# Sums, attributes and maxima moved for four chunks at a time in a four-layer graph network on one core

## What is computed

```
h = x @ enc_node_w + enc_node_b
e = edge_attr @ enc_edge_w + enc_edge_b
def _genconv(h, edge_attr, src, dst, w1, b1, g1, bb1, w2, b2, t):
    msg = jax.nn.relu(h[src] + edge_attr) + EPS_MSG
    m = msg * t
    seg_max = segment_max(m, dst)
    ex = jnp.exp(m - seg_max[dst])
    denom = segment_sum(ex, dst)
    agg = segment_sum(msg * ex / (denom[dst] + 1e-16), dst)
    z = relu(layernorm(((h + agg) @ w1 + b1), g1, bb1))
    return z @ w2 + b2
h = _genconv(h, e, src, dst, ...)
for i in range(1, 4):
    h = h + _genconv(relu(layernorm(h)), e, src, dst, ...)
```

## Time and profile before

| what | us |
|---|---|
| median of three runs (4375.16 to 4376.1) | 4375.87 |
| the profiled execution | 4376.27 |
| its span in the profile | 4374.4 |
| TensorE busy | 2449.6 |
| VectorE busy | 2876.2 |
| ScalarE busy | 1756.3 |
| GpSimd busy | 3117.8 |

### The profile page before, as it was taken

One profiled execution on the slowest core, in us unless ns is written; L12 is line 12 of the kernel. 1 busy time (PEld: TensorE's weight loads), 2 busy tenths in 40 slices (PEclk: granted clock), 3 DMA queues, 4 the chain that ended last, 5 costly groups with the idle time before them and its releaser, 6 DMA issues.

```text
span 4374.4 us, 37023 instructions
## 1 busy us (share of the span) xinstructions
PE 2449.6 (56%) x9731; PEld 1795.5 (41%) x9731; DVE 2876.2 (66%) x3974; ACT 1756.3 (40%) x3407; POOL 3117.8 (71%) x3248
## 2 busy tenths in 40 slices
PE   4566666665455555555455555555555555555554
PEld 3455545554333333333343333333343333333334
DVE  5777777776566666666656666666665666666665
ACT  2444444444334333333333333333333333333334
POOL 3777777777477777777557777777755777777773
PEclk8767677767577776667657666766656676667775
DMA  3444444454233333333223333333322333333332
GB/s 90 133 133 134 139 138 134 133 140 139 86 99 103 108 103 108 104 108 104 94 59 104 108 104 108 103 109 103 108 76 71 108 104 108 104 108 103 108 103 64
DMA packets 307120, 469.62 MB, mean 107 GB/s; under 512 B 169423, under 2 KB 175305, under 8 KB 306892
## 3 DMA queue, kind: packets, MB, share of 16 engines
q1 hardware_dynamic: 200286, 356.83, 23.8%
q0 software_dynamic: 103552, 109.52, 12.4%
q10 hardware_dynamic: 3054, 0.71, 0.1%
HBM read 217.93 MB, written 248.86 MB: 107 GB/s over the span
## 4 chain that ended last, share of the span: by engine, by line
POOL 70%; issue 23%; PE 2%; DVE 2%; DMA 1%; ACT 1%; POOLq 0%; DVEq 0%; ACTq 0%; SPq 0%
POOL zsrc L518 69%; POOL node_sw L529 1%; DMA zsrc<-z_rows,idx_all 1%; PE pT L789 0%; PE pR L886 0%; PE pX L867 0%; PE pX L778 0%; PE pX L711 0%; ACT sq L642 0%; DVE z L1284 0%; DMA node_sw<-sw_rows,row_idx 0%; DMA sw_rows<-sw_out 0%; DMA x_in<-in_x_dram 0%; ACT sw_out L611 0%; DMA z_rows<-z 0%
## 5 line engine op out<-in xcount | busy, mean ns | idle before, releaser
L518 POOL DMA_INDIRECT zsrc<-z_rows,idx_all x3136 | 3019.5, 963 | 1089.0 <-issue 980.1
L778 PE MATMUL pX<-ident,zsrc 128*128 128x128 f32 x2368 | 604.9, 436 | 1296.7 <-DMA zsrc<-z_rows,idx_all 1296.7
L778 PEld LDWEIGHTS pX<-ident,zsrc 128*128 128x128 f32 x2368 | 518.1, 322 | 1595.3 <-DMA zsrc<-z_rows,idx_all 1595.1
L611 ACT ACTIVATE sw_out<-pT 128x512 f32<-128x512 f32 x784 | 424.8, 594 | 1777.5 <-PE pT L789 1773.3
L1108 DVE TENSOR_TENSOR_SCAN S<-decay,S,pX 128x512 f32<-128x512 f32 x296 | 378.6, 1279 | 678.7 <-ACT decay L603 675.0
L789 PE MATMUL pT<-ident,S 128*128 128x128 f32 x1568 | 637.8, 410 | 43.1 <-DVE W L1112 43.1
L789 PE MATMUL pT<-ident,W 128*128 128x128 f32 x1568 | 627.6, 404 | 0.0
L1091 DVE TENSOR_TENSOR_SCAN M<-pR,M,u 128x512 f32<-128x512 f32 x296 | 377.0, 1274 | 286.7 <-ACT u L598 286.7
L596 ACT ACTIVATE r<-pX,edge_b 128x512 f32<-128x512 f32 x296 | 204.8, 692 | 567.0 <-PE pX L778 567.0
L778 PE MATMUL pA<-ident,zsrc 128*128 128x128 f32 x768 | 194.2, 433 | 422.3 <-DMA zsrc<-z_rows,idx_all 422.3
L773 PE MATMUL pX<-attr_pair,edge_w 128*128 128x512 f32 x592 | 416.0, 791 | 12.3 <-ACT attr_pair L590 12.2
(11 more groups left out here) (201 smaller groups left out, 3100.0 us busy)
## 6 DMA issues: line engine op xcount, KB each, us to landing
sw_rows<-sw_out SPq DMA_DIRECT2D x392, 512.0 KB, 2.9
attr_pair<-attr_cols SPq DMA_DIRECT2D x153, 512.0 KB, 4.4
zsrc<-z_rows,idx_all POOLq DMA_INDIRECT x3136, 2.5
attr_in<-in_edge_attr_dram SPq DMA_DIRECT2D x196, 128.0 KB
attr_cols<-attr_pair SPq DMA_DIRECT2D x49, 512.0 KB, 3.2
max_cols<-M SPq DMA_DIRECT2D x49, 256.0 KB, 3.3
z_rows<-z SPq DMA_DIRECT2D x25, 125.0 KB
node_sw<-sw_rows,row_idx POOLq DMA_INDIRECT x100, 2.5
```

What stands on the lines that cost most here:

```text
L518: pool.indirect_dma_start(zsrc[c % RING][:, t4, h, :], None, z_rows, bass.IndirectOffsetOnAxis(idx_all[:, h, t4, c:c + 1].bitcast(U32), 0) ...
L611: act.activation(sw_out[c % 2][:, :, 2 * b:2 * b + 2, :, :].rearrange("p h t s c -> p (t s) h c"), pT[b][:, :].rearrange("p (a h c) -> p a ...
L778: last = pe.matmul(messages_bank(c, first_layer)[:, t4:CH:SUB], zsrc[c % RING][:, t4, :, :].rearrange("p h c -> p (h c)"), ident[:, :], st ...
```

## The change

Stores of sums cover four chunks: sw_out is two buffers of four chunks, 16 KB per partition, and sw_rows is laid out so that a partition's 16 KB are contiguous. The last group has two chunks (98 = 24 x 4 + 2), which are stored one by one, each with 4 KB per partition; the unused half of that group is written once, in layer 0. Attributes are stored and loaded for four chunks (8 KB per partition) in a ring of three such buffers in place of seven pairs, and the maxima of layer 0 are stored for four chunks from an M of four chunks. The loads of the first three groups for the next layer are issued in `end_layer`, behind the seam's two small loads and ahead of the stores of z, after every layer and the last one too. ScalarE waits for a free sums buffer once per four chunks. The row numbers of last edges follow the new layout, which takes more small VectorE operations in node_ends_3. Some scratch tensors of the start now lie in sw_out and xn.

```diff
-attr_pair = [sb(f"attr_pair{b}", [P, 2 * CH]) for b in range(PRING)]
+attr_four = [sb(f"attr_four{b}", [P, FOUR * CH]) for b in range(ARING)]
-M = two("M", [P, 2 * CH + 1])
+M = two("M", [P, FOUR * CH + 1])
-sw_out = two("sw_out", [P, 2, SUB, 2, H])
+sw_out = two("sw_out", [P, FOUR, 2, SUB, 2, H])
...
+            def store_sw(g0, f):
+                sp.wait_ge(back_sb, 2 * g0 + 2 * (FOURS[f][-1] + 1 + PRE))
+                sp.dma_start(sw_four[f, :, :, :].rearrange("p q x -> p (q x)"),
+                             sw_out[f % 2][:, :, :, :, :, :].rearrange("p q h t s c -> p (q h t s c)")).then_inc(sw_stored[f % 2], 16)
...
-                    if c % 2:
-                        q = c // 2
+                    f = c // FOUR
+                    if c == FOURS[f][-1]:
                         sp.wait_ge(attr_sb, c + 1)
-                        sp.dma_start(attr_cols[q, :, :], attr_pair[q % PRING][:, :]).then_inc(cols_stored[q % PRING], 16)
-                    elif c >= 2:
-                        store_m(0, c // 2 - 1)
-                    if c >= 2:
-                        store_sw(0, c - 2)
-
-                for q in range(PAHEAD):
-                    sp.wait_ge(cols_stored[q], 16 * PUSES)
-                    sp.wait_ge(x_mm, done(2 * (NPAIR - PRING + q) + 1))
-                    load_cols(q)
+                        n = len(FOURS[f]) * CH
+                        sp.dma_start(attr_cols[f, :, 0:n], attr_four[f % ARING][:, 0:n]).then_inc(cols_stored[f % ARING], 16)
+                    if c % FOUR == 1 and f >= 1:
+                        store_m(0, f - 1)
+                        store_sw(0, f - 1)
...
             def next_layer(g0):
-                for c in range(NCH):
-                    if c % 2 == 0:
-                        sp.wait_ge(x_mm, done(g0 + (c - 1)))
-                        load_cols((c // 2 + PAHEAD) % NPAIR)
-                    if c >= 2:
-                        store_sw(g0, c - 2)
+                for f in range(1, NF):
+                    if f + ARING - 1 < NF:
+                        sp.wait_ge(x_mm, done(g0 + FOURS[f - 1][-1]))
+                        load_cols(f + ARING - 1)
+                    store_sw(g0, f - 1)
...
                 sp.dma_start(seam_sw1[:, :], seam_row_ap).then_inc(seam_in, 16)
+
+                for f in range(ARING):
+                    if first_layer_end:
+                        sp.wait_ge(cols_stored[f], 16 * A_USES[f])
+                    load_cols(f)
...
                 def copy_out(c):
-                    act.wait_ge(sw_stored[c % 2], q0 * 16 + (c // 2 + 1) * 16)
+                    f, q = c // FOUR, c % FOUR
+                    if q == 0:
+                        act.wait_ge(sw_stored[f % 2], value(act, l * (16 * SW_STORES[f % 2])) + 16 * (f // 2 + 1))
...
-                        v.tensor_copy(kept_max[:, c:c + 1], m[:, bass.ds(seam_cols[c % 2], 1)])
+                        v.tensor_copy(kept_max[:, c:c + 1], m[:, bass.ds(seam_cols[c % FOUR], 1)])
```

More of the change, by code:

```diff
@@ L55 @@
 USES = [len(range(b, NCH, RING)) for b in range(RING)]
-NPAIR = NCH // 2
-PRING = 7
-PUSES = NPAIR // PRING
-assert PUSES * PRING == NPAIR
-PAHEAD = PRING - 1
-M_STORES = ((NPAIR + 1) // 2, NPAIR // 2)
+FOUR = 4
+NF = (NCH + FOUR - 1) // FOUR
+FOURS = [range(f * FOUR, min((f + 1) * FOUR, NCH)) for f in range(NF)]
+ARING = 3
+A_USES = [len(range(b, NF, ARING)) for b in range(ARING)]
+M_STORES = [len(range(s, NF, 2)) for s in range(2)]
+LAST_AT = (NCH - 1) % FOUR * CH
+SW_STORES = [len(range(s, NF - 1, 2)) + (len(FOURS[-1]) if (NF - 1) % 2 == s else 0) for s in range(2)]
+assert EMPTY_ROW == NF * FOUR * 2 * CH
 HOT_AT = 2
@@ L470, in _ @@
             sp.wait_ge(z_stored, 16 * NG * (L + 1))
-            for b in range(PRING):
-                sp.wait_ge(cols_loaded[b], 16 * ((L - 1) * PUSES + (1 if b < PAHEAD else 0)))
+            for b in range(ARING):
+                sp.wait_ge(cols_loaded[b], 16 * ((L - 1) * A_USES[b] + 1))
             sp.wait_ge(out_stored, 16 * NG)
@@ L1150, in whole, with rows_of_edges @@
                     dve.drain()
-                    v.tensor_scalar(out_ap, out_ap, -ROUND, float(n), ALU.add, ALU.mult)
+                    v.tensor_scalar(out_ap, out_ap, -ROUND, float(times), ALU.add, ALU.mult)
                     dve.drain()
+                def rows_of_edges(row, j, part):
+                    first = j
+                    for n, times in ((SUB, 2 * SUB * FOUR - SUB), (CH, 2 * SUB - 2 * CH * FOUR), (CH * FOUR, 2 * CH * FOUR - 2 * SUB * FOUR)):
+                        whole(part, j, n, times)
+                        v.tensor_tensor(row, part, first, ALU.add)
+                        dve.drain()
+                        first = row
                 def node_ends_3():
@@ L1215, in layer @@
                     seam_col_at = dve.value_load(seam_end[0:1, 3:4], min_val=0, max_val=CH - 1)
[L1217 removed]
+                    seam_cols = [value(dve, seam_col_at + (q * CH + 1)) for q in range(FOUR)]
                 last_s = (NCH - 1) % 2
```

128 lines of the change are left out of this document (70 added, 58 removed).

## The result

The changed kernel took 4384.17 us (median of 16 runs, 4377.35 to 4385.74) against 4375.65 for the kernel before (16 runs, 4372.04 to 4377.92): a ratio of 1.0017, 95% interval [1.001, 1.0024], 8.5 us longer. The forecast was 4393, so the sign and the range hold, and the size is half of what was forecast. The profiled execution has a span of 4382.6 us against 4374.4, which is 8.2 of the 8.5.

The account below looks back on a forecast made before the run. The prediction took GpSimd's issuing of the source-row gathers, with the exposed seams between layers, to bound the kernel. Four seams (14.4 us) plus layer 0's last gather (3.0) gave 4375.87 + 17.4 = 4393 us, range 4379 to 4408.

Parts of the forecast that it names:

- the sign: Whole kernel: the change makes it slower, above 4384.6 us, given a chance of 0.78.
- the range: Whole kernel: the time after the change lies between 4379 and 4408 us.
- the size: Whole kernel: 17.4 us longer, 14.4 over four seams between layers and 3.0 at layer 0's last gather.

## What to carry to other kernels

A transfer issued beside the gathers on which an exposed stretch hangs delays them. Here it was about 3 us with 3.15 MB of loads, the same with 6.3 MB, and 5.5 to 7 us with 3.15 MB of stores just ahead of the last gather. What is left at the end is less where the groups behind had waits of their own: follow every group's wait, not only the first's, before summing. Move such transfers behind the last exposed gather, or hold them for it; here the traces give 3.3 us for the one and 6.4 us for the other. When a diff widens a buffer, look for every operation that touches its full width ahead of the first step of the chain.

## What the runs showed of the hardware

- Behind a full SP queue of loads a gather's first packet came 4.1 to 4.6 us after its issue in the seam of layer 1 (1.65 us without loads), after 1.45 to 1.64 MB of SP's bytes, whether 3.15 or 6.3 MB were queued and whether packets had 4 or 8 KB. At the end of layer 0 it was 5.7 us and 1.81 MB before the change, 6.5 us and 2.13 MB after it.
- One fetch of a block of instructions, 1.5 to 1.7 us behind a gather's issue, cost it 0.5 to 0.7 us (3.13 against 2.47 us in layer 1), and it moved out of the way with 64 idle instructions. Here that was 2 us of the drains, half a per mille of the time, for an edit that computes nothing.
- The clearing of 128 x 1025 and 128 x 2049 float elements on VectorE took 0.91 and 1.77 us, and the pause ahead of the operation grew with it, 0.16 and 0.38 us.
- SP's queue alone reached 405 GB/s with 8 KB packets in the seam (1.64 MB in 4.05 us).
